# FFN weight preparation moved from its own stage into eleven rounds of the attention stage of a decoder layer

## The reference

```python
x = x + attention(layernorm(x))           # 16 heads of 32, causal softmax
x = x + mixer(ctx, ctx, layernorm(x))     # 32 heads: causal long convolution of products k_i*v_j
                                          # by 512 taps per head (by FFT in the reference), times q
x = x + ffn(layernorm(x))

def _ste(v, axis):                        # value used: round(v/scale)*scale, scale = max|v|/127 of a row
    ...
xq  = _ste(x, axis=-1)
w1q = _ste(w_gate_up, axis=-1)            # w_gate_up: 2816 rows of 512
gate, up = split(xq @ w1q.T)
h   = silu(gate) * up
hq  = _ste(h, axis=-1)
w2q = _ste(w_down, axis=-1)               # w_down: 512 rows of 1408
y   = hq @ w2q.T
```

## Time and profile before

| | us |
|---|---|
| median of three runs | 1298.21 |
| the profiled execution, whole time | 1299.82 |
| its span | 1298.0 |
| attention stage, to the barrier | 0 to 671.8 |
| FFN weight stage | 671.8 to 714.5 |
| mixer and FFN stage | 714.5 to 1298.0 |
| busy: PE, DVE, ACT, POOL | 1148.5, 1002.2, 881.2, 953.9 |

### The profile page before, as it was taken

The page is one execution under the profiler, slowest core; times in us unless marked ns, Lnnn a source line. Parts: engine busy times, 40 slices in busy tenths (PEclk is TensorE's granted clock), DMA queues, the critical chain, the costliest instruction groups (busy, mean ns, idle before and its releaser), DMA issues. The chain is left out here.

```text
span 1298.0 us, 33415 instructions
## 1 busy us (share of the span) xinstructions
PE 1148.5 (88%) x10020; PEld 816.5 (63%) x10082; DVE 1002.2 (77%) x3160; ACT 881.2 (68%) x1821; POOL 953.9 (73%) x1048
## 2 busy tenths in 40 slices
PE   4779999999999999999766799999999999999985
PEld 3566776766767776677534566666666666666652
DVE  4467877777787777787659588898888888888972
ACT  4477877777787777778737266666667666666654
POOL 1157766766776676767743699999999999999972
PEclk9879999999999999999675899999999999999996
DMA  6244655555445555444455434444444444344400
GB/s 197 74 154 122 208 180 175 174 184 157 138 159 177 177 175 185 157 136 144 164 195 181 125 123 130 134 137 137 137 137 128 126 118 127 130 131 135 130 26 25
DMA packets 87840, 186.57 MB, mean 144 GB/s; under 512 B 12176, under 2 KB 28816, under 8 KB 87760
## 3 DMA queue, kind: packets, MB, share of 16 engines
q1 hardware_dynamic: 86896, 185.02, 44.7%
q10 hardware_dynamic: 864, 0.66, 0.2%
HBM read 105.86 MB, written 54.61 MB: 124 GB/s over the span
## 5 line engine op out<-in xcount | busy, mean ns | idle before, releaser
L625 ACT ACTIVATE prob<-masked,negmax 128x128 f32<-128x128 f32 (+1 forms) x512 | 206.4, 454 | 68.1 <-DVE negmax L754 66.5
L754 DVE CUSTOM_DVE_ANT_0 masked<-s_ps,mask_f 128x128 f32<-128x128 f32 (+1 forms) x512 | 161.1, 351 | 34.7 <-issue 27.7
L997 PE MATMUL y_ps<-kv,toep 128*128 128x288 f16 x640 | 184.8, 289 | 1.4 <-DVE prod L1333 1.4
L998 PE MATMUL y_ps<-kv,toep 128*128 128x288 f16 x640 | 184.4, 288 | 0.0
L999 PE MATMUL y_ps<-kv,toep 128*128 128x288 f16 x640 | 184.3, 288 | 0.0
L388 POOL TENSOR_TENSOR kv_f<-c_in 128x1024 f32<-128x1024 f32 x64 | 143.8, 2247 | 38.8 <-DMA c_in<-in_ctxr 38.8
L760 DVE TENSOR_TENSOR pT_lo<-t_ps,pT_hi 128x384 f16<-128x384 f32 x256 | 140.8, 550 | 40.5 <-ACT pT_hi L633 40.3
L1053 PE MATMUL f_ps<-w1T,xiT 128*128 128x512 bf16 (+1 forms) x736 | 168.5, 364 | 2.7 <-ACT xiT L1174 0.9
L1232 POOL TENSOR_TENSOR tree<-prod 128x512 f32<-128x512 f32 x128 | 163.1, 1274 | 1.3 <-DVE prod L1333 1.3
L1181 ACT ACTIVATE silu<-gate,sx 128x512 f32<-128x512 f32 (+1 forms) x96 | 66.0, 688 | 139.8 <-DVE gate L1387 139.8
L395 POOL TENSOR_TENSOR kv_s<-kv_f,kv_s 128x1152 f16<-128x1152 f32 x64 | 152.2, 2379 | 4.2 <-ACT kv_s L639 3.9
(11 more groups left out here) (156 smaller groups left out, 3532.6 us busy)
## 6 DMA issues: line engine op xcount, KB each, us to landing
kv_pairs<-kv_s SPq DMA_DIRECT2D x64, 576.0 KB, 3.9
kv<-kv_pairs SPq DMA_DIRECT2D x32, 1152.0 KB, 8.0
c_in<-in_ctxr SPq DMA_DIRECT2D x64, 192.0 KB, 3.5
x_in<-in_x SPq DMA_DIRECT2D x16, 512.0 KB, 6.5
q_st<-q_hi SPq DMA_DIRECT2D x128, 64.0 KB, 2.0
k_st<-k_hi SPq DMA_DIRECT2D x128, 64.0 KB, 2.0
x_res<-in_x SPq DMA_DIRECT2D x16, 512.0 KB, 6.8
x_after_attention<-x_out SPq DMA_DIRECT2D x16, 512.0 KB, 5.4
```

Of the source, the lines that this page charges most:

```text
L625: ins = nc.scalar.activation(prob[h % 2][:, at:at + w], masked[h % 2][:, at:at + w], ACT.Exp, bias=negmax[:, h % 2, t:t + 1], scale=-1.0)
L754: ins = nc.vector.tensor_tensor_reduce(masked[h % 2][:, at:at + w], s_ps[h % 2][:, at:at + w], mask_f[:, S - w:S], -1.0, FAR, ALU.add, ALU ...
L997: nc.tensor.matmul(dst, toep[p][:, 0, taps], c[:, 0, m], start=mt == 0, stop=False)
L998: nc.tensor.matmul(dst, toep[p][:, 0, taps], c[:, 1, m], start=False, stop=False)
```

## The change

The stage `ffn_weights` is deleted. In its place:

- In rounds 2 to 12 of attention there are three jobs W, of which each takes a bank and four fp32 transposes of PE: W0 and W1 for one block of 128 rows of w_gate_up each, W2 for 128 columns of w_down (its four row blocks). They stand in `ROUND` at steps 5, 7 and 12. DVE moves each out, with the subtraction of 1.5 * 2^23, into bf16 `w_out`. ACT has no part in moving them out.
- Ahead of them in the same round DVE takes the maxima of the two row blocks behind step 1 and the scales behind step 2, ACT scales and rounds both blocks behind step 3 (ahead of `pairs_high`), and GpSimd scales the columns (four instructions) between `norm` and `pairs(i, 1)`.
- SyncE loads each round's 256 rows and 128 columns one round ahead, between `store_pairs(i-1, 3)` and `stack` (512 KB and 256 KB), and stores the 384 KB of `w_out` to DRAM behind `store_pairs(i, 1)`.
- The row maxima of w_down, which W2 needs, are taken in rounds 0 and 1 (two in each, 128x1408 elements), from four loads of 704 KB.
- The scales go to DRAM at the end of attention: two DMAs of single floats, 2816 and 512 of them. The load of 2 MB of w_gate_up after round 1 goes.
- `w_raw` stays allocated, and the first mixer head's products and taps are loaded into it after round 13.
- In the mixer SyncE loads turned weights and scales (6.03 MB) in round 0; PE and DVE wait for all four loads at the start of round 2. `w1T` is laid out by blocks, so that a moving operand of `gate_up` is read in runs of 128 columns.
- The hardware loop covers rounds 2 to 11 in place of 2 to 13.

```diff
-ROUND = [("QK", 0, 1, 0, 1), ("QK", 1, 1, 2, 3), ("QK", 2, 1, 4, 5), ("QK", 3, 1, 6, 7), ("A", 0, -1, 8, 8), ("V", 0, 1, 8, 9),
-         ("A", 1, -1, 10, 10), ("V", 1, 1, 10, 11), ("X", 0, 2, 12, 12), ("X", 1, 2, 13, 13),
+ROUND = [("QK", 0, 1, 0, 1), ("QK", 1, 1, 2, 3), ("QK", 2, 1, 4, 5), ("W", 0, 0, 5, 5), ("QK", 3, 1, 6, 7), ("W", 1, 0, 7, 7),
+         ("A", 0, -1, 8, 8), ("V", 0, 1, 8, 9), ("A", 1, -1, 10, 10), ("V", 1, 1, 10, 11), ("W", 2, 0, 12, 12),
+         ("X", 0, 2, 12, 12), ("X", 1, 2, 13, 13),
          ("O", 0, -1, 13, 14), ("O", 1, -1, 14, 15)]
+W0, W1 = 2, 13
+W2_MAXIMA, W2_SCALES = ((9, 13), (5, 7)), 9
...
+            def load_w(i, p):
+                if isinstance(i, int) and i < W0 + 2:
+                    sp.wait_ge(w2_max_done, DT)
+                else:
+                    sp.wait_ge(g_free, jobs_before(i - 1))
+                sp.dma_start(w_blk[p], w1[bass.ds((i - W0) * (2 * P), 2 * P)].rearrange("(t p) d -> p t d", p=P)).then_inc(blk_in[p], 16)
+                sp.dma_start(w_col[p], w2[:, bass.ds((i - W0) * P, P)].rearrange("(n p) c -> p n c", p=P)).then_inc(col_in[p], 16)
+            def store_w(i, p):
+                sp.wait_ge(g_free, jobs_before(i) + 1 + max(n for n, j in enumerate(round_jobs(i)) if j[0] == "W"))
+                sp.dma_start(wd[bass.ds(i - W0, 1)].rearrange("r p c -> p (r c)"),
+                             w_out[p][:].rearrange("p k c -> p (k c)")).then_inc(w_stored[p], 16)
...
+            sp.dma_start(sd[0:2 * (W1 - W0)].rearrange("n p -> p n").unsqueeze(2), w_scale[:].unsqueeze(2),
+                         allow_slow_non_contiguous=True).then_inc(scales_stored, 16)
...
+            def columns_scaled(i, p):                                          # gpsimd
+                for n in range(DT):
+                    ins = nc.gpsimd.tensor_scalar(w_col[p][:, n, :], w_col[p][:, n, :], w2_inv[:, n:n + 1], MAGIC, ALU.mult, ALU.add)
...
+                if name == "W":                                                # tensor
+                    pe.wait_ge(*((blk_scaled, i - W0 + 1) if m < 2 else (col_scaled, i - W0 + 1)))
+                    for t in range(DT):
+                        src = w_blk[p][:, m, t * P:(t + 1) * P] if m < 2 else w_col[p][:, t, :]
+                        mm = nc.tensor.transpose(bank[:, t * P:(t + 1) * P], src, eye_f[:])
...
+            def block_scaled(i, p):                                            # scalar, s == 3
+                for k in range(2):
+                    ins = nc.scalar.activation(w_blk[p][:, k, :], w_blk[p][:, k, :], ACT.Copy, bias=MAGIC, scale=w_inv[:, k:k + 1])
...
+                if name == "W":                                                # vector, low()
+                    nc.vector.tensor_scalar(w_out[p][:, m, :], bank[:], MAGIC, None, ALU.subtract).then_inc(g_free, 1)
+            def block_maxima(i, p):                                            # vector, s == 1
+                nc.vector.tensor_reduce(w_max[:], w_blk[p], AX_X, ALU.max, apply_absolute_value=True).then_inc(w_max_done, 1)
+            def block_scales(i):                                               # vector, s == 2
+                nc.vector.tensor_scalar(cols, w_max[:], 1.0 / QMAX, EPS_Q, ALU.mult, ALU.max).then_inc(w_scale_done, 1)
+                nc.vector.reciprocal(w_inv[:], cols).then_inc(w_inv_done, 1)
...
+    def load_weights(sp):                                                      # mixer, round 0
+        sp.dma_start(s1_b[:], ...); sp.dma_start(w1T[:]..., wd[...]); sp.dma_start(w2T[:], wd[...]); sp.dma_start(s2_b[:], ...)
...
+                if isinstance(r, int) and r == 2:                              # mixer, tensor and vector
+                    pe.wait_ge(w_loaded, 64)
...
-def ffn_weights(nc, w1, w2, w1T, w2T, s1_b, s2_b, half_neg2, eps2,
-                eye_f, eye_b, w_raw, OT1, OT2, first_loads):
```

More of the change, by code:

```diff
@@ L105, in hi_before @@
 def hi_before(i):
-    return count_before(i, lambda jobs: sum(j[0] != "O" for j in jobs))
+    return count_before(i, lambda jobs: sum(j[0] not in "OW" for j in jobs))
 def first_bank(i):
@@ L330, in body @@
                 store_pairs(i, 1)
+                if has(jobs, "W"):
+                    store_w(i, p)
+                if isinstance(i, int) and i == W1:
+                    sp.wait_ge(g_free, jobs_before(i))
+                    sp.wait_ge(taps_stored, 16)
+                    for half in range(2):
+                        sp.wait_ge(kv_stored[half], 16)
+                    first_conv(sp)
                 if has(jobs, "O"):
@@ L420, in body @@
                     norm(i + 2)
+                if has(jobs, "W"):
+                    columns_scaled(i, p)
                 pairs(i, 1)
```

286 lines of the change are left out of this document (123 added, 163 removed).

## The result

The changed kernel takes 1322.22 us (median of 4 runs, 1322.09 to 1322.75), the kernel before 1298.38 (4 runs, 1296.14 to 1298.87). The ratio is 1.0187 with a 95% interval of 1.0174 to 1.0200: slower by 1.9%, where 1295.5 was forecast. (The medians of this document leave out one slow execution among all, 6453 us in run 12.) The profiled execution has a span of 1320.4 us, 22.4 over the 1298.0 of before, and its rows place the difference.

The account below looks back on a forecast made before the run. Attention rounds were taken as bound by a chain through SyncE's store and ACT and DVE, the weight stage by DVE. Terms -39.3 - 1 + 31 + 2 + 1.5 + 3.5 = -2.3 led to 1295.5 us, range 1278 to 1313.

Parts of the forecast that it names:

- Its own limit: Attention rounds 2 to 12: output stores 40.9 us apart; the prediction is wrong if under 39.5 or over 42.
- The bank rotation: Steps 8 to 15: V0 waits 1.4 us, O0 some 1.0; PE 0.3 over its margin, counted as 0.
- the first rival: V0 at step 8, O0 at step 13: late banks lengthen each round by up to 1.3 us, +14, 1309; chance 0.20.
- PE's 0.27 + 1.42 us: PE's waits for stacked keys and for pT_lo in step 1, taken as 1.69 us free for additions in steps 8 to 15.
- the forecast of 31 us in eleven rounds: Chain of ACT and DVE in steps 1 to 7: 0.9 + 1.33 + 0.61, sum 2.8 us per round; bounds +14 to +50.
- The preparation: Steps 1 to 7 of each round: maxima and scales add 0.9 us, ACT's two scalings 1.33.
- Rounds 0 and 1: Four maxima of 128x1408 on DVE: round 0 hides two, round 1 grows, +2 (0 to +3); dropped 2 MB load -1.
- The float stores: Two DMAs of 3328 single floats at the end of attention: +1.5 us, with +8 kept for the range.
- Mixer: Weight stage and its cover gone: -42.7 plus 3.4 exposed input loads, net -39.3; weights loaded in mixer round 0: +3.5 (0 to +9).
- The clock: Each of eleven rounds: PE at 1.2 GHz for 5 us behind each of two pauses, +27, 1322; chance 0.08.
- Idle time takes it: Rounds 2 to 12: ACT's and DVE's idle time absorbs their additions, only PE's 1.3 us remains, 1279; chance 0.17.
- Late transfers: Float stores hold the barrier by 8 us, weights hold mixer round 2 by 9; 12 more than counted, 1307; chance 0.12.

Follow-up runs that it names:

- run 12: Changed kernel with W1 at step 11, W2 at 15, preparation moved earlier, scales turned on chip, w2T loaded a mixer round later, loop over two rounds: 1291.66 us.
- the jobs alone: Changed kernel without maxima, scales and both ACT scalings; the three W jobs, their moves, loads and stores stay: 1300.68 us.
- the other order: W1 moved to step 11 and W2 to step 15: changed kernel 1315.66 us; the same without maxima, scales and ACT scalings 1289.64 us.
- the two loops of four: Hardware loop over four attention rounds in place of two: changed kernel 1321.91 us, kernel before 1311.3 us.
- the written-out forms: Hardware loop over attention rounds written out in full: changed kernel 1317.53 us, kernel before 1304.15 us.
- measured alone: Changed kernel without the three W jobs, with the bank rotation of the kernel before; maxima, scales, scalings, loads and stores stay: 1300.97 us.
- run 8: Changed kernel with maxima and scales at steps 0 and 1 ahead of pT_lo, ACT's scaling at step 3 ahead of the exponentials: 1308.88 us.
- Run 9: Changed kernel with scales turned by one PE transpose and stored by one DMA of 26 rows of 512 bytes: 1317.44 us.
- run 7: Changed kernel with w2T and its scales loaded in mixer round 1 and waited for in round 3: 1317.88 us.
- the cured one: Changed kernel with the other bank order, moved preparation, turned scales and weights in two parts: 1291.66 us with the loop over two rounds, 1285.70 us written out.
- run 3: Changed kernel with the two stores of single-float scales moved from the end of attention to the end of round 13: 1327.51 us.
- run 10: Changed kernel with rounds 2 and 3 written out and the hardware loop over four rounds in place of two: 1321.91 us.
- (14): Changed kernel without maxima, scales and both ACT scalings, with the hardware loop over four rounds: 1297.74 us.
- (11): Changed kernel with W1 at step 11, W2 at 15, preparation moved earlier, scales turned on chip, w2T loaded a mixer round later, loop over four rounds: 1289.83 us.
- (13): Kernel before with the hardware loop over four rounds (4 to 11), rounds 12 and 13 written out: 1311.3 us.

## Why the prediction was wrong

The forecast had the wrong sign and was off by 26.7 us. Its own limit, stores more than 42 us apart, was passed too: 463.2 / 11 = 42.1. Step by step:

- **The bank rotation, the step that failed.** "0.3 over, which the chain on ACT does not feel, its own margin being 2.98. I count 0 (to +1.3 each round, the first rival)". The waits came where they were named: V0 for k_lo (1.4 forecast, 1.69 in round 8), O0 for w_out (1.0 forecast, 0.87). Both margins were misread. PE's 0.27 + 1.42 us at the head of the round didn't pay for them in the whole change, since just these steps became waits for DVE (1.40, 2.14, 1.09 above). And ACT does feel them: in the jobs alone its 2.98 us shrink to 0.48. The jobs, counted at 0.61 a round or 6.7 us with 0 for the banks, took 18.5, and the other order takes 8.8 of that off. That margin was not free, because in every second round it was the cover of the next item.
- **DVE's stand at the jump, in no term of the sum.** 3.58 us before, nearly all of it under ACT's wait. With the wait used up it stands bare: the jobs alone cost 0.2 us in an odd round and 4.4 in an even one, and 0.68 a round when written out, against 0.61 forecast. For the whole change the forecast of 31 us in eleven rounds meets 44.8 with the loop, 36.6 between the two loops of four, and 32.0 between the written-out forms (some 3 more by the medians). The terms were sized about right for a round without a jump.
- These two overlap. The other bank order alone takes 7.3 us off the rounds of the change and 8.8 off the jobs alone, and the jump's part is 10.5 to 12.8; they are no shares of one sum.
- **The preparation.** 2.2 x 11 = 24.5; measured alone 21.6. The term was right. What the prediction took as given was its place: moved, as in run 8, it costs 11.7 us less in the rounds.
- **Both halves together** cost 4.7 more than apart by the rounds and 2 less by the medians. The prediction added its terms, and nothing clear of noise speaks against that.
- **Rounds 0 and 1:** +4.2 against +1. No run took the four w2 maxima away, so the cause stays open.
- **The float stores:** 5.9 against 1.5, the high end of 8 being nearer. The Trainium skill's "DMA: Bandwidth & Descriptors", Rules for kernel authors, says that a last dimension that isn't contiguous becomes one descriptor per element, and the trace agrees that such stores are slow. The choice near zero was wrong: 3328 floats took 15.5 and 18.2 us. The prediction also named "over 15 us" as what would prove it wrong. Run 9 mends it.
- **Mixer:** -32.9 against -35.8. Exposed input loads 4.4 (3.4 counted), weights some 5.4 (3.5 counted): 593.3 - 626.2 + 42.7 - 4.4. Its mechanism was right, head 2's products queued behind 6 MB, and run 7 took it away.
- **Rivals.** The clock: its 1322 us hit by chance. It wanted 5 us at 1.2 GHz in each of eleven rounds; the rows have some 3.5 us in four of them, three times right behind V0's wait of 1.69 us. Round 8 has the same wait and stays at 1.00. PE's busy time puts it at 4.8 us in all, not 27, and at 1.5 us in the kernel before (round 3). So it is another way, a small one, in which the bank waits cost time. Idle time takes it: true in the odd rounds of the jobs alone (37.8 against 37.6), false for the sum. Late transfers: 4.4 + 1.9 of the 12 us. Bank rotation: its waits are real and worth 7 to 9 of its 14 us, but they act by way of ACT's margin, in the jobs alone together with the jump, and not by PE's 1.69 us alone.

The Trainium skill, "Runtime: NRT & Kernel Launch", Instruction fetch mechanics, says that a taken branch breaks the sequential prefetch, that it stalls where its target isn't in the part already held, and that kernels prefer full unrolling partly for this. The rows agree that an engine can stand at a jump, DVE for 2.1 to 4.6 us; that it waits for instructions there is shown by no run. The preference doesn't hold everywhere here: written out, the kernel before lost 0.4%, the changed one gained 4.7 us of 1322 (intervals overlap) and the cured one 6.0 of 1292.

What stays open: rounds 0 and 1, how far the bank waits hurt without a jump, what the clock's four falls cost apart from the waits that they follow, and why ACT's wait for the product store, and with it the round, grows when the code is written out.

## What to carry to other kernels

Before you set added waits against an idle time, ask what else that idle time covers: another added term, or a stall of another engine at the same moment, such as one marked "issue" at a loop head, which costs little until the cover is spent (here 0.5 us in an even round) and then adds to the round (4.4). A new job in a rotation of buffers changes who follows whom, so cost the list and try its other orders. Measure cures one at a time, and add up only what was measured: here the sum came out within 2 us. And turn a store of scattered single elements on chip first: here 13 KB took up to 18 us to land and moved the barrier by 5.9.

## What the runs showed of the hardware

- Two stores of 2816 and 512 single floats landed after 15.5 and 18.2 us, and in rounds 13 and 14 of run 3 they lengthened the round by 8.3 and 5.2 us.
- Two DMA issues took 8.42 and 6.41 us on SyncE behind 4.2 and 5.6 MB of weights and scales, where single ones in these rows mostly take 0.4: the next head's loads waited in SyncE and not in the queue.
- With a loop over two rounds DVE stands 2.1 to 4.6 us behind every jump back in attention, and PE and ACT don't. With a loop over four rounds, at its one jump, PE stood 4.54 (run 10), 4.88 (14) and 2.49 us (11), ACT 2.88 (13) and 4.18 us (11), and DVE 4.18 (14) and 3.10 us (11). Written out, no stand in rounds 3 to 12 reaches 2 us.
- Behind V0's wait of 1.69 us the granted clock fell to half for some 3.5 us in rounds 3, 6 and 7 of the changed kernel, and stayed at 1.00 in round 8.
- The page's part 3 lists 28 instruction packets (0.46 MB) on queue 8 before and 59 (0.97 MB) with the rounds written out, and the median landing of a product store between 250 and 600 us went from 3.9 to 4.5 us. Whether the one causes the other wasn't tried.
